# Expert up products of two mixture-of-experts layers as plain fp32 with 64 rows, two side by side in the row halves of the array

## What is computed

```
layer 0:  n = layernorm(h)            logits = n @ Wg.T + bg
          w = softmax over the two largest logits, 0 elsewhere
          h += sum_e w[e] * (relu(n @ W1[e].T + b1[e]) @ W2[e].T + b2[e])          W1[e]: 256 x 64
layer 1:  n = rmsnorm(x) * ln2_w      logits = n @ router_w.T
          w = the two largest of softmax(logits), divided by their sum
          h += sum_e w[e] * ((silu(n @ w1[e].T) * (n @ w3[e].T)) @ w2[e].T)        w1[e], w3[e]: 170 x 64
```

## Time and profile before

| | |
|---|---|
| median of 3 runs (lowest to highest) | 1184.48 us (1181.44 to 1195.03) |
| the profiled execution's own time | 1186.37 us |
| its span, first to last instruction | 1184.6 us |
| mean granted TensorE clock | 0.945 |
| busy in the span: TensorE, weight loads | 1049.7, 770.0 us |
| busy: VectorE, ScalarE, GpSimd | 866.7, 596.8, 461.6 us |

### The profile page before, as it was taken

How to read it: one execution, slowest core, us unless ns; L and a number is a source line. 1 busy time by engine, 2 the same in 40 slices (tenths; PEclk the granted TensorE clock), 3 DMA queues, 4 the chain that set the end, 5 groups by cost and what they waited for, 6 DMA issues and landing times. The chain is left out here.

```text
span 1184.6 us, 24247 instructions
## 1 busy us (share of the span) xinstructions
PE 1049.7 (89%) x8559; PEld 770.0 (65%) x8559; DVE 866.7 (73%) x2081; ACT 596.8 (50%) x1289; POOL 461.6 (39%) x618
## 2 busy tenths in 40 slices
PE   6795878579999999994879969986999999999995
PEld 2474856457777777772655547763777777878783
DVE  1596969757777777774868679973688888777874
ACT  1274646555565566552324437763545454545451
POOL 2235302203443444344345387734043433333434
PEclk8797999989999999998889989997999999999998
DMA  8200000000000000000000000000000000000000
GB/s 229 108 1 1 3 2 2 1 1 2 1 2 1 1 1 1 1 1 1 1 1 1 1 1 3 2 2 1 1 6 7 7 6 7 12 7 7 7 7 12
DMA packets 3456, 13.59 MB, mean 11 GB/s; under 512 B 400, under 2 KB 2192, under 8 KB 2960
## 3 DMA queue, kind: packets, MB, share of 16 engines
q1 hardware_dynamic: 3056, 8.00, 2.4%
q0 software_dynamic: 288, 4.11, 0.9%
HBM read 9.98 MB, written 2.13 MB: 10 GB/s over the span
## 5 line engine op out<-in xcount | busy, mean ns | idle before, releaser
L1318 PE MATMUL moe_psU<-moe_nT_parts,moe_w_hi 128*128 128x320 f32 x988 | 324.4, 339 | 2.4 <-DVE moe_hid L1228 1.2
L1318 PE MATMUL moe_psU<-moe_nT_parts,moe_w_lo 128*128 128x320 f32 x988 | 296.4, 310 | 0.0
L1318 PEld LDWEIGHTS moe_psU<-moe_nT_parts,moe_w_hi 128*128 128x128 f32 x988 | 187.9, 190 | 57.2 <-issue 50.1
L1318 PEld LDWEIGHTS moe_psU<-moe_nT_parts,moe_w_lo 128*128 128x128 f32 x988 | 188.3, 191 | 0.0
L1222 DVE TENSOR_TENSOR moe_hid<-moe_psU,moe_silu 128x320 f32<-128x320 f32 x286 | 139.3, 491 | 62.1 <-ACT moe_silu L1086 52.6
L1013 POOL TENSOR_TENSOR moe_sum<-moe_scaled 128x256 f32<-128x256 f32 x130 | 99.1, 763 | 171.1 <-DVE moe_scaled L1212 170.5
L1086 ACT ACTIVATE moe_silu<-moe_psU 128x320 f32<-128x320 f32 x286 | 125.5, 439 | 56.5 <-PE moe_psU L1318 40.0
L1091 ACT ACTIVATE moe_hid<-moe_psU,middle 128x320 f32<-128x320 f32 x260 | 129.4, 528 | 33.4 <-PE moe_psU L1318 31.1
L1228 DVE TENSOR_SCALAR moe_hid<-moe_psU,middle 128x320 f32<-128x320 f32 x156 | 85.7, 550 | 64.9 <-PE moe_psU L1318 64.1
L1329 PE MATMUL moe_psY<-moe_hid,late 128*64 128x320 f32 x832 | 123.4, 439 | 0.9 <-DVE moe_hid L1222 0.9
L1329 PE MATMUL moe_psY<-moe_hid,middle 128*64 128x320 f32 x832 | 123.4, 439 | 0.7 <-ACT moe_hid L1091 0.7
(11 more groups left out here) (301 smaller groups left out, 1893.8 us busy)
## 6 DMA issues: line engine op xcount, KB each, us to landing
images<-in_x SPq DMA_DIRECT2D x8, 576.0 KB, 11.6
late<-in_late POOLq DMA_DIRECT2D x1, 2456.5 KB, 11.9
out_tokens<-h SPq DMA_DIRECT2D x13, 160.0 KB, 1.8
middle<-in_middle POOLq DMA_DIRECT2D x1, 1554.0 KB, 6.8
early<-in_early SPq DMA_DIRECT2D x1, 1043.0 KB, 19.9
early<-in_early SPq DMA_DIRECT2D x1, 80.0 KB, 2.0
```

What stands on the lines that cost most here:

```text
L1318: last = pe.matmul(psum[:, 0:HALF], w[:, col:col + SPLIT], moving, start=(part == 0), stop=(part == 1))
```

## The change

The weight sets `w_hi` and `w_lo` and the split of n are gone. VectorE writes n twice, side by side, in one operation over 640 elements (`nrm_twice`); turned, `nT_twice` holds the same n in rows 0 to 63 and in rows 64 to 127. A product is one plain fp32 matmul over 64 rows, straight from the packed weights; two of them are issued one behind the other, the first in rows 0 to 63 of the array, the second in rows 64 to 127: in layer 0 the tiles of two neighbouring units, in layer 1 the up and the gate tile of a unit. Both banks must be free ahead of the first. The logits are plain fp32 over rows 0 to 63, 8 columns. The factor `ln2` goes into ScalarE's copy of the turned n. Layer 1 begins with a one-column silu.

```diff
-        w_hi, w_lo = sb("w_hi", [128, NUP], F32R), sb("w_lo", [128, NUP], F32R)
-        nTr = [sb(f"nT_parts{k}", [128, TOK], F32R) for k in range(2)]
-        nrm, split = sb("nrm", [B, T, D]), sb("split", [B, T, 128])
+        nTr = [sb(f"nT_twice{k}", [128, TOK]) for k in range(2)]
+        nrm = sb("nrm_twice", [B, T, 2, D])
...
-                def high_parts(g):
-                    act.wait_ge(n_set, g + 1)
-                    need(act, T_mm, g * len(TURNS))
-                    act.copy(split[:, :, 0:D].bitcast(F32R), nrm[:, :, :]).then_inc(hi_set, 1)
...
-                high_parts(0)
+                if layer == 1:
+                    act.activation(sil[0][:, 0:1], late[:, c["ln2"]], ACT.Silu).then_inc(silu_table, 1)
+                    act.wait_ge(silu_table, 1)
...
-                    need(dve, lo_set, g)
-                    dve.tensor_tensor(nrm[:, :, :], tile, over_width(stats[:, 2, :]), ALU.mult).then_inc(n_set, 1)
-                    yield
-                    dve.wait_ge(n_set, g + 1)
-                    dve.wait_ge(hi_set, g + 1)
-                    dve.tensor_tensor(split[:, :, D:], nrm[:, :, :], split[:, :, 0:D], ALU.subtract).then_inc(lo_set, 1)
+                    need(dve, T_mm, g * len(TURNS))
+                    dve.tensor_tensor(nrm[:, :, :, :], tile.unsqueeze(2).to_broadcast([B, T, 2, D]),
+                                      stats[:, 2, :].unsqueeze(2).unsqueeze(3).to_broadcast([B, T, 2, D]), ALU.mult).then_inc(n_set, 1)
...
-                        last = pe.matmul(psM[:, at:at + 2 * E], nTr[slot][:, t * B:(t + 1) * B], w_gate[:, :], start=True, stop=True)
+                        last = pe.matmul(psM[:, at:at + E], nTr[slot][0:D, t * B:(t + 1) * B], late[0:D, gate_cols],
+                                         start=True, stop=True)
...
                     if layer == 0:
                         wait_evicted(pe, g, u - 4)
-                        turns = [(psU[u % 4], 0, up_mm)]
+                        wait_evicted(pe, g, u - 3)
+                        turns = [(psU[u % 4], col_of[0, chunk], up_mm), (psU[(u + 1) % 4], col_of[0, units[u + 1][2]], up_mm)]
...
-                        col = col_of[kind, chunk]
-                        for part, w in enumerate((w_hi, w_lo)):
-                            last = pe.matmul(psum[:, 0:HALF], w[:, col:col + SPLIT], moving, start=(part == 0), stop=(part == 1))
-                        last.then_inc(done, 1)
+                    for x, (psum, col, done) in enumerate(turns):
+                        rows, at = slice(D * x, D * x + D), up_cols.start + col
+                        pe.matmul(psum[:, 0:HALF], late[rows, at:at + SPLIT], nTr[slot][rows, half * HALF:(half + 1) * HALF],
+                                  start=True, stop=True).then_inc(done, 1)
...
                     for p, k, u in places():
-                        up(g, slot, u, not before)
+                        if layer == 1 or k % 2 == 0:
+                            up(g, slot, u)
```

More of the change, by code:

```diff
@@ L1059, in keep_transposed @@
                     take_waits(act, act_taken)
-                    act.copy(nTr[slot][:, t0 * B:t1 * B], psM[:, 0:(t1 - t0) * B]).then_inc(nTr_set, 1)
+                    into, turned = nTr[slot][:, t0 * B:t1 * B], psM[:, 0:(t1 - t0) * B]
+                    if layer == 0:
+                        act.copy(into, turned).then_inc(nTr_set, 1)
+                    else:
+                        act.activation(into, turned, ACT.Copy, scale=late[:, c["ln2"]]).then_inc(nTr_set, 1)
                 def exponentials(g):
@@ L1166, in ask_routing @@
                     else:
-                        yield from chain.spread(dve.tensor_reduce(V["m0"], S["val"], axis=AX.X, op=ALU.max))
-                        yield from chain.spread(dve.tensor_tensor(S["d"], S["val"], over(V["m0"]), ALU.subtract))
+                        yield from chain.spread(dve.tensor_reduce(V["m0"], logits_ps, axis=AX.X, op=ALU.max))
+                        dve.tensor_tensor(S["d"], logits_ps, over(V["m0"]), ALU.subtract).then_inc(L_read, 1)
+                        yield
+                        dve.wait_ge(L_read, g + 1)
                         dve.sem_inc(exp_asked, 1)
@@ L1249, in _ @@
                 first = norm(0)
[L1250 to L1265, removed]
                 for _ in first:
@@ L1279, in transposes @@
                     t0, t1 = TURNS[part]
-                    pe.wait_ge(lo_set, g + 1)
+                    pe.wait_ge(n_set, g + 1)
                     need(pe, L_read, g)
@@ L1286, in transposes @@
                     for t in range(t0, t1):
-                        last = pe.transpose(psM[:, (t - t0) * B:(t - t0 + 1) * B], split[:, t, :], ident)
+                        last = pe.transpose(psM[:, (t - t0) * B:(t - t0 + 1) * B],
+                                            nrm[:, t, :, :].rearrange("b x d -> b (x d)"), ident)
                     last.then_inc(T_mm, 1)
@@ L1308, in up @@
+                        turns = [(psU[u % 4], col_of[0, chunk], up_mm), (psU[(u + 1) % 4], col_of[0, units[u + 1][2]], up_mm)]
                     else:
                         need(pe, hid_act, g * ACT_PER + (u - 1))
[L1310 to L1315, removed]
[L1316 to L1319 removed]
+                        before = [v for v in range(u) if gate_bank[v] == gate_bank[u]]
@@ new lines, in up @@
+                        wait_evicted(pe, g, before[-1] if before else
+                                     max(v for v in range(UPG) if gate_bank[v] == gate_bank[u]) - UPG)
+                        turns = [(psU[u % 2], col_of[0, chunk], up_mm), (psU[2 + gate_bank[u]], col_of[1, chunk], gate_mm)]
+                    for x, (psum, col, done) in enumerate(turns):
+                        rows, at = slice(D * x, D * x + D), up_cols.start + col
+                        pe.matmul(psum[:, 0:HALF], late[rows, at:at + SPLIT], nTr[slot][rows, half * HALF:(half + 1) * HALF],
+                                  start=True, stop=True).then_inc(done, 1)
```

43 lines of the change are left out of this document (17 added, 26 removed).

## The result

| | before | after |
|---|---|---|
| median of 4 runs (lowest to highest) | 1184.09 us (1181.44 to 1195.03) | 1261.06 us (1253.30 to 1263.34) |
| the profiled execution | 1186.37 us | 1259.42 us |
| granted clock over the span | 0.945 | 0.943 |

The changed kernel is slower: the ratio is 1.062, 95% interval 1.054 to 1.070. The forecast was 1251.5 (1208 to 1282).

The account below looks back on a forecast made before the run. The prediction took TensorE's stream to bound the mixtures. Its terms, -25 + 60 + 14.6 + 23 - 5.5 = +67, gave 1253.5 us for the profiled execution, 1251.5 beside the median, with 1208 to 1282 for 8 in 10.

Parts of the forecast that it names:

- Up products: Pairs of up products in both layers: 0.54 us a pair side by side instead of 0.59, -25 us over 494 pairs.
- Changes of form: TensorE switching between 64 and 128 rows around token-major blocks and the turn of n: 0.40 us more a block, +60 us.
- Waits in layer 1: Third pair of an unbroken run waits 0.26 us for silu's eviction, four times a group: 13.5 us.
- Waits in layer 0: After the down product, unit 5's late eviction (0.59 more) and the first token-major block (0.23) wait each group: +9.8 us.
- Logits: Five plain fp32 logits products a group load their token columns twice, 0.11 us each: +14.6 us.
- Beginnings: Starts of both layers: the turn of n starts 1.6 and 2.3 us earlier, silu's table about 1: -5.5 us.
- rival C: Changes of form cost about half, as loads for the free array half go ahead: +30 for +60, 1221 us; 8%.
- Rival A: No drain between 64 and 128 rows, only between column forms: 1192 us, or 1169 without waits; 9%.

Follow-up runs that it names:

- same_half: The changed kernel with both products of a pair in rows 0 to 63, so never side by side: 1566.44 us.
- the two opposite runs: Layer 0's token-major blocks as 64-row transposes, in the kernel before (1187.22 us) and in the changed kernel with ScalarE's later read of the down result (1234.62 us).
- read_later: The changed kernel with ScalarE evicting unit 5 ahead of reading the down result in layer 0: 1257.88 us, 25.27 us a group of layer 0.
- mixed: Layer 0 changed, all in 64-row form, later read, logits one pair earlier; layer 1 as before plus early silu: 1180.68 us, ratio 0.9948 to before.

## Why the prediction was right

The direction and the mechanism held, and the groups came out at 26.03 and 28.98 us where 26.0 and 29.4 were forecast. That layer 0 agrees to 0.03 us is in part luck: five blocks and the turn were priced 0.4 too high and the waits 0.4 too low. In layer 1, where the waits were right, the first error stands alone.

- **Up products.** 0.54 a pair, as taken from the earlier trace rows; the outer bound of 1.08 was the true price without the overlap, as same_half showed.
- **Changes of form, the largest term.** They cost, in both kernels, and go when the form stays. The size was too high: 0.40 more a block was forecast. Measured in layer 1, two pairs and a block hold 1.28 + 0.58 = 1.86 us, less 2 x 0.54 is 0.78 for 0.84; before it was 0.45: +0.33. The step that was off is the load ahead of the first transpose: 0.11 was entered, but in the trace the starts in the block are 0.165, 0.11 and 0.11 apart, with 0.20 to the next product, so the load cost 0.055. 120 blocks at 0.07 too much are 8 us. The 0.30 of the two opposite runs is the same price from another side.
- **Waits in layer 1.** 0.25 for 0.26, four times a group, and gone where the run is broken.
- **Waits in layer 0.** 0.82 more a group was forecast, about 1.2 measured. The place after the last down product was right (0.84 forecast, 0.91 over the run of three), and so was the first token-major block (0.23 forecast; it starts 1.01 behind the down product where 0.74 is free running, and 0.03 of the 0.27 comes back in the block: 0.24). Missed was that blocks don't cover the wait wholly: two of them are followed by a wait of 0.15 each, which was gone in read_later. Together 1.45, less the 0.25 of before. And of the 0.91 only a part was the order of ScalarE; 0.45 stayed in read_later, the plain time from a pair to its banks, a term that the sum had for layer 1 and not for layer 0.
- **Logits.** 0.56 a group, confirmed alone.
- **Beginnings.** -1.9 and -2.6 to the first up product, for -1.6 and -2.3. But layer 0's first products run at a clock of 0.59 after and 0.68 before, and from the first up product to the first down product it is 9.6 us for 8.5, which gives 1.1 back. The further 1 us for silu's table is not borne out (mixed).

The sum said +67 for the profiled execution and +73 came: +37.4 in layer 0 (34 in the sum), +33.1 in layer 1 (33), +2.6 outside both, where the code is the same and the clock was not. The other 3.5 us to the median lie in which execution was profiled: it is 1.6 below its median where before's was 1.9 above. Half a drain per change (rival C) is not what the blocks show: 0.33 of the 0.40 is there, 0.30 by the estimate from the two opposite runs. Rival A falls by the same numbers.

## What to carry to other kernels

Running small plain products side by side in the array came out level here only when what stood between them kept the same form: count the changes of form in the stream, not only the products' own time, and convert the small transposes between them too, if there are banks for both halves. A pair that ends as a whole holds its banks for its results and one eviction: with banks for two pairs, set something else between every second and third pair. Compare periods of a loop and not totals, when the clock differs in code that nobody touched.

## Not expected of the hardware

- Transposes of 64 rows by 64 columns, two at a time, follow each other by 0.06 us, the full ones by 0.11: eight hold 0.24 us and four 0.44.
- With the up products in one row half, the clock fell to 1.2 GHz around one down product of each group (granted clock 0.59 over the 3.84 us of one), in a stream in which TensorE was busy throughout; it is 1.00 in the steady groups with both halves in use. No run here tells why.
- Swapping which of the two engines evicts which tile of a pair hardly changes the wait (2.17 and 2.20 us for three pairs).
